# Attention: the products with ones of a key tile stand directly behind its value products, and not a step later

## The chip, the cores and the metric

The kernel runs on one core of a Trainium2 chip. The metric is the device time of one execution in microseconds (us), and the median of several runs is taken.

## The reference

A transformer block on x of 2 x 2048 x 512 in float32: x plus attention of the normalised x, and then a mixture of experts with a shared expert, which the change doesn't touch. What matters here is the attention, with 16 heads of 32 columns:

```python
scores = jnp.einsum('bhqd,bhkd->bhqk', q, k) / jnp.sqrt(jnp.float32(DH))
causal = jnp.tril(jnp.ones((s, s), dtype=bool))
scores = jnp.where(causal[None, None], scores, -jnp.inf)
attn = jax.nn.softmax(scores, axis=-1)
out = jnp.einsum('bhqk,bhkd->bhqd', attn, v)
```

## The kernel before

The program has three phases: projections (to about 275 us of the profiled execution), attention (to about 1435 us) and the experts. The order on every engine is written out by hand; semaphores tie the engines together.

Attention goes over 8 groups of four heads (`NG`; called rounds below). In a round it goes over four units, the query chunks q = 0 to 3 of 512 queries, and in a unit over the key tiles of 128 keys in the order `ORDER[q]`. A tile is two steps, one for each pair of heads, so there are 640 steps for 320 tiles. The last four key tiles by number of a unit (kt from 4q on) are diagonal tiles, which need the causal mask; `ORDER` spreads them among the full ones.

A step n of TensorE (PE) holds two score products (`score(n, 0)` and `score(n, 1)`, L1011, keys by queries, into one of three banks `b_st`), a share of the items of a stream (mostly L988: scores in the other orientation, queries by keys, into three banks `b_mx`, for the row maxima of a later unit), in thirds around the others, and in its middle one of two things:

- in odd steps, from the third on, the value group of the tile before, `values(m)`, L1024: four heads, each 32 columns wide in the array, side by side; a record of the trace says x8, since each head's float32 product is two instructions. It accumulates into the bank `b_ob`.
- in even steps the ones group of the same tile, `count_ones(m)`, L1038: the same exponentials (`b_pt`) multiplied by ones, which gives the softmax's row sums, into `b_sb`. It exists for 18 of a round's 40 tiles (`ONES_TILES`); for the others (`POOL_TILES`) GpSimd adds the exponentials up (L752), and at a unit's end `finish` (L1046) brings that sum into `b_sb`.

The other engines in a step: ScalarE (ACT) makes the exponentials of both scores (L931, `b_pt<-b_st`, eight buffers). On a diagonal tile both wait for VectorE (DVE), which adds the mask after both scores of the step are there (L893, or L897 in two pieces, `b_st<-b_st,b_sooner`). In DVE's order the mask stands behind the maxima (L871, L868) of the step's items of the first two thirds. PE's score number i (two to a step) waits until the exponential of number i - 3 has left the bank, and `values(m)` waits for the last exponential of its tile. ACT copies `b_sb` out for the unit that ended (L952) two or four steps into the next, and the first ones group of a unit waits for that copy (`s_sev`).

```python
ORDER = ((0, 1, 2, 3), (0, 1, 4, 2, 5, 3, 6, 7), (0, 1, 2, 8, 3, 4, 9, 5, 6, 10, 7, 11),
         (0, 1, 2, 12, 3, 4, 5, 13, 6, 7, 8, 14, 9, 10, 11, 15))
ONES_TILES = ((0, 1, 2, 3), (2, 6, 7), (2, 9, 6, 10, 11), (2, 4, 13, 8, 14, 15))
FINISH = (2, 4, 4, 2)
```

A group's width in columns is 512, less 128 for each tile that a diagonal tile lies behind the first diagonal one.

Of the kernel before, what the change touches and what calls it, by code (L numbers as in the profile page):

```python
# [604 lines left out]
def phase_attention(nc, x, w, scratch, ahead, keep, heads):  # L605
# [9 lines left out]
    NS, NU = len(steps), len(units)  # L615
# [22 lines left out]
    def item_shares(n):  # L638

        here, there = upto[n - 1] if n else start, upto[n]  # L640
        return [here + (there - here) * k // 3 for k in range(4)]
# [20 lines left out]
    def unit_ending(n, offset):  # L662

        for u in range(NU):
            if first_step[u + 1] + (offset[units[u][1]] if isinstance(offset, tuple) else offset) == n:
                return u
        return None

    with ExitStack() as ctx:
# [51 lines left out]
        with nc.Block() as block:  # L721
# [138 lines left out]
            def _(v):  # L860
                def partial_max(i):
                    _, u, t, h, c = stream[i]
                    q = units[u][1]
                    w = min(CH, (TPC * q + t + 1) * P - c * CH)
                    v.wait_ge(s_item, i + 1)
                    part = mpart[u % 2][:, t, h, c:c + 1]
                    if c == q:
                        v.tensor_tensor_reduce(unread[i % NMX][:, 0:w], mxb[i % NMX][:, 0:w], later[:, CH - w:], 1.0, -3e38,  # L868
                                               ALU.add, ALU.max, part).then_inc(s_red, 1)
                    else:  # L870
                        v.tensor_reduce(part, mxb[i % NMX][:, 0:w], AX.X, ALU.max).then_inc(s_red, 1)  # L871
                    if (t, h, c) == (TPC - 1, HG - 1, q):
                        v.wait_ge(s_red, maxes_before[i + 1])
                        v.tensor_reduce(mt[u % 2][:, :, 0:MROW + 1:DH], mpart[u % 2][:, :, :, 0:q + 1],
                                        AX.X, ALU.max, negate=True).then_inc(s_mcol, 1)
# [24 lines left out]
                for n in range(NS):  # L900
                    here, _, some, there = item_shares(n)
                    for i in range(here, some):
                        if stream[i][0] == "max":
                            partial_max(i)
                    if steps[n][2] >= TPC * steps[n][1]:
                        mask(n)
                    for i in range(some, there):
                        if stream[i][0] == "max":
                            partial_max(i)
                    if n == first_step[NQ * NG - 2]:  # L910
                        v.wait_ge(s_sum, 16)
                        v.reciprocal(rsum[:], sums[:]).then_inc(s_rec, 1)
# [57 lines left out]
            def _(pe):  # L970
                def item(i):
                    what = stream[i]
                    bank = mxb[i % NMX]
                    if i >= NMX:
                        if stream[i - NMX][0] == "max":
                            pe.wait_ge(s_red, maxes_before[i - NMX + 1])
                        else:
                            pe.wait_ge(s_turn, stream[i - NMX][1] + 1)
                    if what[0] == "max":
                        _, u, t, h, c = what  # L980
                        it, q = units[u]
                        w = min(CH, (TPC * q + t + 1) * P - c * CH)
                        if (t, h, c) == (0, 0, 0):
                            pe.wait_ge(s_q[q], 48 * (it + 1))
                        if (t, h) == (0, 0) and c == q:
                            pe.wait_ge(s_k[c][it % 2], 48 * (it // 2 + 1))
                        at = key_slot(it, c) * CH
                        ins = pe.matmul(bank[:, 0:max(w, 2 * P)], qb[0:KR, h, q * CH + t * P:q * CH + (t + 1) * P],  # L988
                                        kb[0:KR, h, at:at + max(w, 2 * P)], start=True, stop=True)
                        ins.then_inc(s_item, 1)  # L990
                    else:
                        u = what[1]
                        pe.wait_ge(s_mcol, u + 1)
                        for t in range(TPC):
                            ins = pe.transpose(bank[0:MROW + 1, t * P:(t + 1) * P], mt[u % 2][:, t, :], ident[:])
                        ins.then_inc(s_item, 1)

                def score(n, j):
                    u, q, kt, p = steps[n]
                    it = units[u][0]  # L1000
                    d = kt - TPC * q
                    lo = min(max(d, 0) * P, 2 * P)
                    if 2 * n + j >= NST:
                        pe.wait_ge(s_exp, 2 * n + j - NST + 1)
                    if n == first_step[2] and j == 0:
                        pe.wait_ge(s_rest, 1)
                    if n == first_step[u] and j == 0:
                        pe.wait_ge(s_row[q], 16 * (it + 1))
                    at = key_slot(it, kt // TPC) * CH + kt % TPC * P
                    h = 2 * p + j  # L1010
                    pe.matmul(stb[:, (2 * n + j) % NST, lo:], kb[:, h, at:at + P],  # L1011
                              qb[:, h, q * CH + lo:(q + 1) * CH], start=True, stop=True).then_inc(s_st, 1)

                def values(m):
                    u, q, kt, _ = steps[2 * m]
                    it = units[u][0]
                    lo = max(kt - TPC * q, 0) * P
                    pe.wait_ge(s_exp, 4 * m + 4)
                    if kt == ORDER[q][0] and u:
                        pe.wait_ge(s_oev, u)  # L1020
                    if q == kt // TPC and kt % TPC == 0:
                        pe.wait_ge(s_v[q], 16 * (it + 1))
                    for h in range(HG):
                        ins = pe.matmul(ob[h * DH:(h + 1) * DH, lo:], vbuf[:, kt, h * DH:(h + 1) * DH],  # L1024
                                        pt[(2 * m + h // 2) % NPB][:, h % 2, lo:],
                                        start=(kt == ORDER[q][0]), stop=(kt == ORDER[q][-1]))
                    ins.then_inc(s_pv, 1)

                def count_ones(m):
                    u, q, kt, _ = steps[2 * m]  # L1030
                    if kt in POOL_TILES[q]:
                        return
                    lo = max(kt - TPC * q, 0) * P
                    begin = ONES_TILES[q][0]
                    if kt == begin and u:
                        pe.wait_ge(s_sev, u)
                    for h in range(HG):
                        ins = pe.matmul(sb[h * DH:(h + 1) * DH, lo:], ones[:],  # L1038
                                        pt[(2 * m + h // 2) % NPB][:, h % 2, lo:],
                                        start=(kt == begin), stop=(kt == ORDER[q][-1] and not POOL_TILES[q]))  # L1040
                    ins.then_inc(s_one, 1)

                def finish(u):
                    pe.wait_ge(s_add, pool_total(u))
                    for h in range(HG):
                        ins = pe.matmul(sb[h * DH:(h + 1) * DH, :], ones[:], acc[summed.index(u) % 2][:, h],  # L1046
                                        start=False, stop=True)
                    ins.then_inc(s_fin, 1)
# [6 lines left out]
                for n in range(NS):  # L1055
                    here, *some = item_shares(n)
                    score(n, 0)
                    for i in range(here, some[0]):
                        item(i)
                    if n % 2 == 0 and n >= 4:  # L1060
                        count_ones((n - 4) // 2)
                    if n % 2 and n >= 3:
                        values((n - 3) // 2)
                    for i in range(some[0], some[1]):
                        item(i)
                    score(n, 1)
                    for i in range(some[1], some[2]):
                        item(i)
                    done = unit_ending(n, FINISH)
                    if done is not None and done in summed:  # L1070
                        finish(done)
                values(NS // 2 - 1)
                count_ones(NS // 2 - 2)
                count_ones(NS // 2 - 1)
                finish(NU - 1)

# [1079 lines left out]
```

## Time and profile before

| | |
|---|---|
| median of 3 runs | 2293.08 us (2290.29 to 2299.49) |
| profiled execution, time | 2301.97 us |
| profiled execution, span | 2300.3 us |
| TensorE matmul busy | 2139.7 us, 93% |
| VectorE busy | 1483.7 us, 64% |
| GpSimd busy | 1168.6 us, 51% |
| ScalarE busy | 1034.7 us, 45% |
| mean granted TensorE clock | 0.974 of full speed |

Busy time of an engine is the union of its instructions' durations. Ends of matmuls are modelled in the trace, so distances in this document are taken from start to start. A time in brackets in a row of the timeline is the idle time of the engine before it, and behind it stands what ended it. The change touches attention alone, which takes 1160 of the 2300 us.

### The profile page before, as it was taken

Reading aid. Unit: us, or ns where it says so; the run is one execution under the profiler, and the core shown is the slowest. Engines: PE = TensorE matmul, PEld = TensorE weight load, DVE = VectorE, ACT = ScalarE, POOL = GpSimd, SP = SyncE. Lnnn points to the kernel's source line nnn. Section 1 sums busy time; section 2 is a strip of 40 time slices with the busy share of each in tenths; the row PEclk is TensorE's granted clock in tenths of the full one; section 3 lists DMA queues with packets and bytes.
Section 4 is the critical chain, followed back from the end, with each engine's and each line's share of the span. In section 5 each row is a group of like instructions: output and inputs, shape, how many; then the busy total and the mean of one; then the engine's idle time right before and its main releaser. Section 6 shows DMA issues by size and latency. Waiting matters only on the chain. (4 is left out here: it accounts for less than half of the span.)

```text
span 2300.3 us, 32737 instructions
## 1 busy us (share of the span) xinstructions
PE 2139.7 (93%) x11865; PEld 1389.3 (60%) x11865; DVE 1483.7 (64%) x3323; ACT 1034.7 (45%) x1924; POOL 1168.6 (51%) x717
## 2 busy tenths in 40 slices
PE   6999899999999999999999988699998899999997
PEld 5777544444444444444444432577776798999896
DVE  3665786767767677777777760765657556565654
ACT  3333255555555555555555555322222334443433
POOL 1010166557465674656746557455563345465554
PEclk9999799999999999999999999899999899999999
DMA  5678711412213122161231200344432676767673
GB/s 169 233 264 257 194 31 38 93 33 69 67 38 93 29 67 72 38 153 29 68 71 38 73 17 19 124 147 129 147 111 80 235 242 196 237 227 249 215 225 115
DMA packets 172913, 283.69 MB, mean 123 GB/s; under 512 B 28622, under 2 KB 75214, under 8 KB 172752
## 3 DMA queue, kind: packets, MB, share of 16 engines
q1 hardware_dynamic: 151488, 219.09, 32.5%
q0 software_dynamic: 21264, 62.51, 8.2%
q8 instruction: 94, 1.54, 0.3%
q14 instruction: 67, 0.55, 0.1%
HBM read 196.22 MB, written 86.90 MB: 123 GB/s over the span
## 5 line engine op out<-in xcount | busy, mean ns | idle before, releaser
L931 ACT ACTIVATE b_pt<-b_st 128x512 f32<-128x512 f32 (+3 forms) x1280 | 612.5, 535 | 472.7 <-DVE b_st L893 187.6
L752 POOL TENSOR_TENSOR b_acc<-b_acc,b_pt 128x1024 f32<-128x1024 f32 (+1 forms) x256 | 592.9, 2346 | 214.3 <-ACT b_pt L931 213.7
L871 DVE TENSOR_REDUCE b_mpart<-b_mx 128x1 f32<-128x512 f32 x768 | 512.1, 686 | 184.8 <-PE b_mx L988 182.1
L1011 PE MATMUL b_st<-b_q,b_k 97*128 97x512 f32 (+2 forms) x1280 | 497.4, 402 | 57.5 <-ACT b_pt L931 54.0
L988 PE MATMUL b_mx<-b_k,b_q 96*128 96x512 f32 (+2 forms) x1280 | 508.9, 412 | 6.9 <-DVE b_mpart L871 3.3
L988 PEld LDWEIGHTS b_mx<-b_k,b_q 96*128 96x128 f32 x1280 | 248.4, 195 | 262.0 <-DVE b_mpart L871 148.9
L1011 PEld LDWEIGHTS b_st<-b_q,b_k 97*128 97x128 f32 x1280 | 242.3, 191 | 262.7 <-ACT b_pt L931 237.4
L1024 PE MATMUL b_ob<-b_pt,b_v 128*32 128x512 f32 (+3 forms) x2560 | 303.6, 547 | 1.1 <-ACT b_pt L931 1.1
L868 DVE CUSTOM_DVE_ANT_0 b_unread<-b_mx,b_later 128x384 bf16<-128x384 f32 (+3 forms) x512 | 244.5, 484 | 87.0 <-PE b_mx L988 86.3
L752 POOL TENSOR_TENSOR b_acc<-b_pt 128x1024 f32<-128x1024 f32 x48 | 113.5, 2379 | 263.0 <-ACT b_pt L931 263.0
L80 PE MATMUL c_fb<-e_w_split,e_xh 128*128 128x352 f32 x408 | 142.3, 349 | 1.4 <-DVE e_xl L1727 1.4
L2015 ACT ACTIVATE c_hh<-e_tb 128x384 fp32r<-128x384 f32 x71 | 34.9, 491 | 230.4 <-PE e_tb L2065 187.6
L82 PE MATMUL c_fb<-e_w_split,e_xh 128*128 128x352 f32 x408 | 133.2, 326 | 0.0
L81 PE MATMUL c_fb<-e_w_split,e_xl 128*128 128x352 f32 x408 | 133.0, 326 | 0.0
L893 DVE TENSOR_TENSOR b_st<-b_st,b_sooner 128x256 f32<-128x256 f32 x171 | 73.1, 428 | 65.8 <-PE b_st L1011 65.6
L1038 PE MATMUL b_sb<-b_pt,b_ones 128*32 128x512 f32 (+3 forms) x1152 | 114.9, 471 | 0.0
L2042 DVE TENSOR_TENSOR c_hl<-e_tb,c_hh 128x384 fp32r<-128x384 f32 x71 | 39.5, 557 | 102.8 <-ACT c_hh L2015 97.6
L1024 PEld LDWEIGHTS b_ob<-b_pt,b_v 128*32 128x32 f32 x2560 | 50.6, 108 | 90.0 <-issue 46.4
L1981 POOL DMA_INDIRECT out_dram<-c_x,entry x36 | 50.5, 1403 | 83.0 <-DVE c_x L2030 52.1
L1412 POOL DMA_INDIRECT scr_table<-c_entry,c_slot x64 | 75.1, 1173 | 25.2 <-issue 18.0
L1981 POOL DMA_INDIRECT out_dram<-c_x1k,entry x35 | 45.4, 1297 | 71.1 <-DVE c_x1k L2030 29.0
L1451 ACT ACTIVATE c_sg<-c_fb 128x512 f32<-128x512 f32 (+1 forms) x24 | 14.3, 597 | 147.2 <-PE c_fb L82 139.6
(296 smaller groups left out, 3818.0 us busy)
## 6 DMA issues: line engine op xcount, KB each, us to landing
b_q<-scr_qh SPq DMA_DIRECT2D x64, 256.0 KB, 4.5
b_k<-scr_kh SPq DMA_DIRECT2D x64, 256.0 KB, 4.1
sw_raw<-in_L_ffn_w_gate_dram SPq DMA_DIRECT2D x14, 704.0 KB
sw_raw<-in_L_ffn_w_up_dram SPq DMA_DIRECT2D x14, 704.0 KB
c_x_rows<-in_L_ffn_w_gate_dram SPq DMA_DIRECT2D x13, 704.0 KB
c_x_rows<-in_L_ffn_w_up_dram SPq DMA_DIRECT2D x13, 704.0 KB
a_xin<-in_L_attn_x_dram POOLq DMA_DIRECT2D x8, 1024.0 KB, 5.8
scr_qh<-wo SPq DMA_DIRECT2D x8, 1024.0 KB, 5.0
```

Source lines behind the costliest of these rows:

```text
L80: nc.tensor.matmul(out, wh, xh, start=first, stop=False)
L81: nc.tensor.matmul(out, wl, xh, start=False, stop=False)
L82: return nc.tensor.matmul(out, wh, xl, start=False, stop=last)
L752: g.tensor_tensor(out[:, :, lo:], so_far[:, :, lo:], pt[n % NPB][:, :, lo:], ALU.add).then_inc(s_add, 1)
L868: v.tensor_tensor_reduce(unread[i % NMX][:, 0:w], mxb[i % NMX][:, 0:w], later[:, CH - w:], 1.0, -3e38, ALU.add, ALU.max, part).then_inc(s_ ...
L871: v.tensor_reduce(part, mxb[i % NMX][:, 0:w], AX.X, ALU.max).then_inc(s_red, 1)
L931: act.activation(pt[n % NPB][:, j, lo:], stb[:, (2 * n + j) % NST, lo:], ACT.Exp, scale=SCALE).then_inc(s_exp, 1)
L988: ins = pe.matmul(bank[:, 0:max(w, 2 * P)], qb[0:KR, h, q * CH + t * P:q * CH + (t + 1) * P], kb[0:KR, h, at:at + max(w, 2 * P)], start=Tr ...
L1011: pe.matmul(stb[:, (2 * n + j) % NST, lo:], kb[:, h, at:at + P], qb[:, h, q * CH + lo:(q + 1) * CH], start=True, stop=True).then_inc(s_st, 1)
L1024: ins = pe.matmul(ob[h * DH:(h + 1) * DH, lo:], vbuf[:, kt, h * DH:(h + 1) * DH], pt[(2 * m + h // 2) % NPB][:, h % 2, lo:], start=(kt == ...
L1038: ins = pe.matmul(sb[h * DH:(h + 1) * DH, lo:], ones[:], pt[(2 * m + h // 2) % NPB][:, h % 2, lo:], start=(kt == begin), stop=(kt == ORDER ...
L1981: g.indirect_dma_start(out=out, in_=rows[i % RING], out_offset=at, in_offset=None, bounds_check=T - 1, oob_is_err=False).then_inc(s_sc, 16)
```

## The change

On PE the ones group of a tile leaves the even step and stands in the odd step before it, directly behind the tile's value group. Nothing is added or left out: 143 of the 144 ones groups move, and the last one of all stood there already. No other engine's order changes, and neither do the waits, the buffers or the shares of items that each step gets.

```diff
@@ -1057,10 +1057,9 @@
                     score(n, 0)
                     for i in range(here, some[0]):
                         item(i)
-                    if n % 2 == 0 and n >= 4:
-                        count_ones((n - 4) // 2)
                     if n % 2 and n >= 3:
                         values((n - 3) // 2)
+                        count_ones((n - 3) // 2)
                     for i in range(some[0], some[1]):
                         item(i)
                     score(n, 1)
@@ -1070,7 +1069,6 @@
                     if done is not None and done in summed:
                         finish(done)
                 values(NS // 2 - 1)
-                count_ones(NS // 2 - 2)
                 count_ones(NS // 2 - 1)
                 finish(NU - 1)
```

PE's order in the third round, unit q = 0, from the value group of tile 0 on, as it was. `b_ob` takes value groups, `b_sb` ones groups, `b_st` scores and `b_mx` items.

```order
L1024 MATMUL b_ob<-b_pt0,b_v 32x512 x2
L1024 MATMUL b_ob<-b_pt1,b_v 32x512 x2
L988 MATMUL b_mx2<-b_k,b_q 128x512
L1011 MATMUL b_st<-b_q,b_k 128x384
L988 MATMUL b_mx0<-b_k,b_q 128x512
L1011 MATMUL b_st<-b_q,b_k 128x256
L1038 MATMUL b_sb<-b_pt0,b_ones 32x512 x2
L1038 MATMUL b_sb<-b_pt1,b_ones 32x512 x2
L1011 MATMUL b_st<-b_q,b_k 128x256
L988 MATMUL b_mx1<-b_k,b_q 128x512
L1011 MATMUL b_st<-b_q,b_k 128x256
L1024 MATMUL b_ob<-b_pt2,b_v 32x384 x2
```

The same place of PE's order after the change.

```order
L1024 MATMUL b_ob<-b_pt0,b_v 32x512 x2
L1024 MATMUL b_ob<-b_pt1,b_v 32x512 x2
L1038 MATMUL b_sb<-b_pt0,b_ones 32x512 x2
L1038 MATMUL b_sb<-b_pt1,b_ones 32x512 x2
L988 MATMUL b_mx2<-b_k,b_q 128x512
L1011 MATMUL b_st<-b_q,b_k 128x384
L988 MATMUL b_mx0<-b_k,b_q 128x512
L1011 MATMUL b_st<-b_q,b_k 128x256 x2
L988 MATMUL b_mx1<-b_k,b_q 128x512
L1011 MATMUL b_st<-b_q,b_k 128x256
L1024 MATMUL b_ob<-b_pt2,b_v 32x384 x2
```

The ones group stood between the second and the third score behind the value group; now the two groups of eight are one block, and those two scores are neighbours.

## Rows read from the trace of the kernel before

**Rows 1.** The page: engine totals, TensorE clock granted in 40 slices of the span.

```profile
PE 2139.7 (93%) x11865; PEld 1389.3 (60%) x11865; DVE 1483.7 (64%) x3323; ACT 1034.7 (45%) x1924; POOL 1168.6 (51%) x717
PEclk9999799999999999999999999899999899999999
```

**Rows 2.** Waits of PE from 270 to 1430 us: total us, times, longest.

```profile
PE b_st L1011 <- ACT b_pt L931: 54.0, 108, 1.2
```

**Rows 3.** The page's groups: all ones groups (eight records each).

```profile
L1038 PE MATMUL b_sb<-b_pt,b_ones 128*32 128x512 f32 (+3 forms) x1152 | 114.9, 471 | 0.0
```

**Rows 4.** Timeline of PE, 706 to 708 us: start, duration, instruction.

```profile
706.04 0.39 PE L1011 MATMUL b_st<-b_q,b_k 97*128 97x512 f32 x1
706.36 1.07 PE L1024 MATMUL b_ob<-b_pt,b_v 128*32 128x512 f32 x8
707.36 0.50 PE L988 MATMUL b_mx<-b_k,b_q 96*128 96x512 f32 x1
707.70 0.40 PE L1011 MATMUL b_st<-b_q,b_k 97*128 97x512 f32 x1
707.93 0.34 PE L988 MATMUL b_mx<-b_k,b_q 96*128 96x384 f32 x1
```

**Rows 5.** Timeline of PE, 703 to 706 us: a ones group of 256 columns.

```profile
704.90 0.64 PE L1038 MATMUL b_sb<-b_pt,b_ones 128*32 128x256 f32 x8
705.47 0.50 PE L1011 MATMUL b_st<-b_q,b_k 97*128 97x512 f32 x1
```

**Rows 6.** Timeline of PE at the end of attention.

```profile
1428.26 0.43 PE L1024 MATMUL b_ob<-b_pt,b_v 128*32 128x128 f32 x8 [1.08 <-ACT b_pt L931]
1428.50 0.40 PE L1038 MATMUL b_sb<-b_pt,b_ones 128*32 128x128 f32 x8
```

**Rows 7.** Timeline, 577 to 581 us, round 3, q = 0, behind tile 0.

```profile
576.99 0.60 ACT L952 ACTIVATE b_sst<-b_sb 128x512 f32<-128x512 f32 x1
577.16 1.06 PE L1024 MATMUL b_ob<-b_pt,b_v 128*32 128x512 f32 x8
...
578.49 0.34 PE L1011 MATMUL b_st<-b_q,b_k 97*128 97x384 f32 x1
...
578.69 0.69 DVE L868 CUSTOM_DVE_ANT_0 b_unread<-b_mx,b_later 128x512 bf16<-128x512 f32 x1 [1.99 <-PE b_mx L988]
...
579.12 1.07 PE L1038 MATMUL b_sb<-b_pt,b_ones 128*32 128x512 f32 x8
...
579.31 0.49 DVE L897 TENSOR_TENSOR b_st<-b_st,b_sooner 128x128 f32<-128x128 f32 x2
...
579.92 0.87 ACT L931 ACTIVATE b_pt<-b_st 128x384 f32<-128x384 f32 x2 [2.33 <-DVE b_st L897]
580.46 0.39 PE L1011 MATMUL b_st<-b_q,b_k 97*128 97x256 f32 x1 [0.27 <-ACT b_pt L931]
```

**Rows 8.** Timeline, 650 to 652 us, q = 2, behind tile 6.

```profile
650.97 2.16 ACT L931 ACTIVATE b_pt<-b_st 128x256 f32<-128x256 f32 x5 [1.53 <-DVE b_st L893]
651.50 0.50 PE L1011 MATMUL b_st<-b_q,b_k 97*128 97x512 f32 x1
```

**Rows 9.** Timeline, 718 to 719 us, behind tile 15 of q = 3.

```profile
718.80 0.45 PE L1011 MATMUL b_st<-b_q,b_k 97*128 97x384 f32 x1 [0.35 <-ACT b_pt L931]
```

**Rows 10.** Windows, 465 to 470 us: length, busy time and count by engine, granted clock, DMA.

```profile
465.00:470.00 5.00, 5.00 (x24) 2.29 (x23) 2.53 (x6) 2.13 (x5) 0.00 (x0) 0.50 0.71 157
```

**Rows 11.** Timeline of PE: the same three tiles in round 2 and round 3.

```profile
463.10 0.39 PE L1011 MATMUL b_st<-b_q,b_k 97*128 97x256 f32 x1 [0.67 <-ACT b_pt L931]
...
463.69 0.64 PE L1024 MATMUL b_ob<-b_pt,b_v 128*32 128x256 f32 x8
...
478.92 1.06 PE L1024 MATMUL b_ob<-b_pt,b_v 128*32 128x512 f32 x8
...
611.78 0.64 PE L1024 MATMUL b_ob<-b_pt,b_v 128*32 128x256 f32 x8
...
622.58 1.06 PE L1024 MATMUL b_ob<-b_pt,b_v 128*32 128x512 f32 x8
```

## The prediction

> **What bounds the kernel now.** I read the page first: TensorE is busy for 93% of the span, VectorE for 64%, ScalarE for 45% [rows 1]. Then the waits of PE within attention: score products wait for ScalarE's exponentials for 54.0 us in 108 waits, and nothing else makes PE wait for more than a few us there [rows 2]. So attention is bound by PE's order. But the 54 us aren't spread evenly, and for this change it matters where they lie. So the third view is the timeline of PE, ScalarE and VectorE together, tile by tile. The rounds repeat each other almost to 0.1 us, so I went through one round (577 to 721 us) and read what stands behind each of its 18 ones groups.
>
> What the reader is to see there is the place behind tile 0 [rows 7]. The value group starts at 577.16. Behind it come an item and a score at 578.49, which is the second score of a diagonal step. Now a chain runs through other engines: VectorE takes the item's maximum (578.69, 0.69 us), then adds the mask (579.31), then ScalarE makes the exponential (from 579.92), and only then may PE write the score that needs this bank (580.46). PE has meanwhile done one more item, one score and the ones group (579.12). It still waits 0.27 us. So the ones group isn't on the path here: it is what PE does while the chain runs.
>
> **The change, part by part.** It removes two changes of shape on PE for each ones group, and it moves the group ahead of the chain.
>
> *What a change of shape costs.* Groups have the form 128\*32, all other products use the full width. Between two plain products of 512 columns the starts are 0.23 us apart (707.70 to 707.93). A plain product ahead of a group takes 0.32 (706.04 to 706.36), 0.09 more. A group of 512 takes 1.00 to the next plain product, and that one takes 0.34 to its successor, 0.11 more [rows 4]. A group of 256 takes 0.57 [rows 5], so 256 columns cost 0.43, and one of 128 would take 0.355 if a plain product followed. At the end of attention a ones group follows a value group of 128 directly, after 0.24 [rows 6]: 0.115 less. So where a ones group stands directly behind its value group, PE's own work is shorter by 0.09 + 0.11 + 0.115 = 0.31 us. The page's 1152 records are 144 groups [rows 3]. The page "TensorEngine Tiling (Array Packing)" of the Trainium skill, section Key Properties, says that changing the tiling mode drains the engine; the trace agrees, with 0.31 us for the way in and out, and by that rule alone the change could only gain.
>
> *What the move costs.* The block of both groups is longer than the value group by what a group takes in front of another one: 1.00 - 0.115 = 0.885 us at 512 columns, 0.67 at 384, 0.455 at 256, 0.24 at 128. All that stands behind the block starts so much later, the item and the second score of the step among them, and with them the chain through mask and exponential. In front of the waiting score there is now no group. So the wait comes to light in full.
>
> I take the 18 places of a round by what comes next. The wait that a place already has, or the slack it has, decides how much of the delay is seen.
>
> - *Four places with a 512 group ahead of a diagonal tile that is the first or second one* (behind tile 0 of q = 0 and tile 2 of the other three units). The score waits for the exponential already, or starts within 0.1 us of its end, as in rows 7. The chain and this score start 0.885 later. The score no longer follows a group, which gives 0.11 back: +0.775 each, 3.10 together. Does another part of the chain absorb some? VectorE had been idle for 1.99 us before the item came [rows 7], so no.
> - *Four places ahead of a later diagonal tile* (tiles 1 and 2 of q = 0, 6 of q = 1, 6 of q = 2). The mask is narrower, and there is slack between the exponential's end and the score. Behind tile 6 of q = 2 the exponentials start at 650.97; one of 256 columns takes about 0.4, so the score at 651.50 was free some 0.09 earlier [rows 8]. That gives 0.885 - 0.09 - 0.11 = +0.685. For the three others, read the same way, slack is 0, 0.05 and 0.05 with groups of 384, 256 and 256: +0.56, +0.295, +0.295. Together 1.84.
> - *Two more places ahead of a diagonal tile* (8 and 15 of q = 3). Here an earlier wait for the exponential of the step before absorbs the delay of the block. Behind tile 15 the later score waits 0.35 anyhow [rows 9], and I count 0. Behind tile 8 the gain in PE's work remains: -0.31.
> - *Eight places ahead of a full tile.* No mask; the exponential is made within the time of the next three scores and their items, also 0.885 later. The gain in PE's work is seen: -0.31 for seven. The eighth (tile 9 of q = 2) has six items, and VectorE's 0.69 for each maximum [rows 7] holds it: I count -0.12. Together -2.29.
>
> A round: 3.10 + 1.84 - 0.31 - 2.29 = +2.34 us; eight rounds: **+18.7 us**. Nothing hides later what was lost: PE's order continues behind the wait as it was.
>
> *Other edges.* The move frees `b_pt` a step earlier; ScalarE doesn't wait for ones groups in any row that I found, so this is worth nothing. The first ones group of a q = 0 unit now meets its wait for ScalarE's copy of the sums: the copy starts at 576.99 and takes 0.60, the ones group would start 0.885 after 577.16, at 578.05, 0.46 after the copy [rows 7]. Queued behind it would be everything of PE. I take 0. The queues of SP and GpSimd aren't moved past.
>
> *Against which time.* The rows come from an execution of 2301.97 us (span 2300.3, 1.7 outside it); with the sum it would take 2320.7. The median of the runs is 2293.08, 8.9 lower. So the forecast is 2293.1 + 18.7 = about 2312 us.
>
> *Bounds.* If the eight gains came without any delay being seen, and -0.31 at all 144, the sum would be -44.6 us. If the gains failed and the delays held, 8 x 4.94 = +39.5. If only half of each delay is seen, 8 x (2.47 - 2.60) = -1.
>
> **The rivals.**
>
> 1. *PE's work is all that counts* (faster). For it: 93% busy, 54 us of waits against 1160, and 0.31 us less work at each of 144 places. Against it: the waits stand just where the groups are moved from. It decides if the chain can be repaid, that is if the time from the block's end to the waiting score is shorter than I read it by more than 0.5 us. Time: 2293.1 - 44.6 = 2248.5.
> 2. *A wash.* The chain is shorter behind a long block, since ScalarE and VectorE have cleared all their older work by then, and half the delay is absorbed. For it: ScalarE still has up to two older exponentials when a value group starts. Against it: VectorE idle for 1.99 and ScalarE for 2.33 us in rows 7. Time: 2293.1 - 1 = about 2292.
> 3. *The clock.* From 465 to 470 us the granted clock is 0.50, the lower level of 1.2 GHz [rows 10], where most of attention has 1.00 (2.4 GHz). Ahead of it PE had waited 0.67 us for an exponential. The stretch from 463.69 to 478.92 takes 15.23 us, the same tiles a round later 10.80 [rows 11]: 4.4 us for one such episode. The page's clock row shows few such slices [rows 1]; read finely, attention has three after its start. The change adds some 32 waits of about a microsecond. If each round got one more episode, that is 8 x 4.4 = 35 us on top: 2347. Against it: behind each long wait there now stands no longer gap than those that the rounds have five times each already, mostly with the full clock. The page "TensorE: Matmul & The Clock Gate", in the section on why this matters for kernels, advises against idle gaps between bursts since the clock falls with them; the trace agrees that the clock falls after a stretch with waits, here one of 0.67 us.
> 4. *The sums' copy is late*, and PE stands at the first ones group of seven q = 0 units. It decides from 0.46 us on; 0.5 us beyond that would be 3.5 us. I count it inside the range and not by itself.
>
> **How the numbers follow.** Forecast as summed, 2301 to 2326: 0.60. Rival 1: 0.10. Rival 2: 0.18. Rival 3: 0.12. The range of eight in ten is 2297 to 2335: below it lie rival 1 and most of rival 2, above it rival 3's larger half. A difference under 0.5%, 11.5 us, is about what a measurement of this kernel can't tell from none; slower by more is the forecast and rival 3 (0.72), within it rival 2 (0.18), faster rival 1 (0.10).
>
> **What the profile of the changed kernel would show.** Right, if a ones group of 512 starts about 0.885 us behind its value group; if PE's waits of scores for exponentials rise from 54 us by some 60 (the delays seen, and the 0.31 at each of these places, which becomes waiting) and stand at the third score behind the blocks ahead of diagonal tiles, 1.1 us more at each of the four places of the first kind; if the distance from the value group of tile 0 to that of tile 1 in q = 0 grows by 0.8, and the one behind tile 14 of q = 3 falls by 0.3; and if a round without a fall of the clock takes about 2.3 us longer. Wrong, if the ones group behind its value group costs more than 0.885 (then it is worse), if the mask starts earlier after the block than the item's maximum lets it (then rival 1 or 2), or if the windows show more than three stretches at half the clock.

## The result, and the profile after

The changed kernel takes 2332.95 us (median of 4 executions, 2328.25 to 2340.85), where the kernel before has 2295.89 beside it: a ratio of 1.0169, 95% interval 1.0137 to 1.0202. That is 31 to 46 us slower; 18.7 were forecast. The profiled execution took 2330.91 us with a span of 2329.2. One execution of all that follow, of the kernel joined ahead of full tiles, took 4129 us at a mean clock of 0.528 and is left out of the ratios.

The page after, engine totals and the clock granted in 40 slices [rows 1]:

```profile
PE 2116.9 (91%) x11865; PEld 1403.3 (60%) x11865; DVE 1474.5 (63%) x3323; ACT 1029.8 (44%) x1924; POOL 1167.7 (50%) x717
PEclk9999799999999999999999999799999899999999
```

Waits of PE in attention after, 270 to 1462 us (total us, times, longest) [rows 2]:

```profile
PE b_st L1011 <- ACT b_pt L931: 109.9, 147, 1.3
```

PE has the same instructions and is busy for 23 us less, and it waits for exponentials for 56 us more; some 60 were forecast. The forty slices don't show the clock's falls, which are a few us long; that comes below.

The place of [rows 7] in the timeline after, behind tile 0 of q = 0 in the third round (start, duration, instruction):

```profile
580.54 0.60 ACT L952 ACTIVATE b_sst<-b_sb 128x512 f32<-128x512 f32 x1
580.72 1.07 PE L1024 MATMUL b_ob<-b_pt,b_v 128*32 128x512 f32 x8
581.60 1.04 PE L1038 MATMUL b_sb<-b_pt,b_ones 128*32 128x512 f32 x8
...
582.91 0.34 PE L1011 MATMUL b_st<-b_q,b_k 97*128 97x384 f32 x1
...
583.11 0.69 DVE L868 CUSTOM_DVE_ANT_0 b_unread<-b_mx,b_later 128x512 bf16<-128x512 f32 x1 [2.85 <-PE b_mx L988]
...
583.73 0.49 DVE L897 TENSOR_TENSOR b_st<-b_st,b_sooner 128x128 f32<-128x128 f32 x2
...
584.33 0.87 ACT L931 ACTIVATE b_pt<-b_st 128x384 f32<-128x384 f32 x2 [3.19 <-DVE b_st L897]
584.88 0.39 PE L1011 MATMUL b_st<-b_q,b_k 97*128 97x256 f32 x1 [1.27 <-ACT b_pt L931]
585.10 0.41 PE L988 MATMUL b_mx<-b_k,b_q 96*128 96x512 f32 x1
...
585.57 0.53 PE L1024 MATMUL b_ob<-b_pt,b_v 128*32 128x384 f32 x4
```

Counted from the start of the value group, the ones group starts at 0.88 (0.885 forecast), and all links of the chain stand 0.85 or 0.86 later than before: the second score at 2.19 (1.33), the mask at 3.01 (2.15), the exponentials at 3.61 (2.76), the waiting score at 4.16 (3.30). PE's own work reaches that score 1.27 us too early. The sums' copy ends at 581.14, before its ones group starts, as forecast.

Since the rounds repeat each other, I compared both traces by places: the distance from one value group's start to the next, for each of a round's 40 tiles, as the median over the rounds. 22 tiles without a ones group: within 0.01 us of before. The 18 with one, in us of change, beside the forecast:

| places of a round | forecast | measured |
|---|---|---|
| 512 columns, ahead of the first or second diagonal tile (4) | +0.775 each, +3.10 | +0.88, +0.89, +0.87, +0.85, together +3.49 |
| ahead of a later diagonal tile (4) | +0.56, +0.295, +0.295, +0.685, together +1.84 | +0.65, +0.31, +0.26, +0.80, together +2.02 |
| behind tiles 8 and 15 of q = 3 | -0.31, 0 | -0.19, +0.01 |
| ahead of a full tile (8) | -2.29 together | -0.34, -0.33, +0.06, -0.08, -0.27, -0.20, -0.21, -0.20, together -1.57 |
| a round | +2.34 | +3.76 |
| eight rounds | +18.7 | +30.1 |

The total attention stretch, first to last value group, grew by 33.5 us (1153.5 to 1187.0). So 30 are in the places; the rest is in rounds that the medians leave out, those with falls of the clock among them. The two other phases are together 4.6 us shorter in this profile than in the one before, which is why the spans differ by only 29.

### The profile page after: what moved, and what is told of

It is laid out like the page before. It is cut to its first block and busy times, and to the rows that moved or that the text cites. A ratio compares the mean times of both kernels' runs of the same rounds, so it can differ in the third digit from the quotient of the medians.

```text
span 2329.2 us, 32737 instructions
## 1 busy us (share of the span) xinstructions
PE 2116.9 (91%) x11865; PEld 1403.3 (60%) x11865; DVE 1474.5 (63%) x3323; ACT 1029.8 (44%) x1924; POOL 1167.7 (50%) x717
## 5 line engine op out<-in xcount | busy, mean ns | idle before, releaser
L1011 PE MATMUL b_st<-b_q,b_k 97*128 97x512 f32 (+2 forms) x1280 | 487.6, 400 | 112.7 <-ACT b_pt L931 109.9
L80 PE MATMUL c_fb<-e_xh,c_sw_guh 128*128 128x512 f32 (+2 forms) x192 | 77.0, 401 | 3.7 <-DVE e_xl L1567 3.7
```

Of the source, the lines that this page charges most:

```text
L80: nc.tensor.matmul(out, wh, xh, start=first, stop=False)
```

## The experiments

All are set against the kernel before, run beside them on the same chip. "Joined" means that a ones group stands directly behind its value group.

**Joined only ahead of full tiles.** `mask_next(m)` says whether the tile after m is diagonal.

```diff
-                    if n % 2 == 0 and n >= 4:
+                    if n % 2 == 0 and n >= 4 and mask_next((n - 4) // 2):
                         count_ones((n - 4) // 2)
                     if n % 2 and n >= 3:
                         values((n - 3) // 2)
+                        if not mask_next((n - 3) // 2):
+                            count_ones((n - 3) // 2)
```

> The ones group joins its value group only where the next key tile is a full one (8 of 18 places of a round); where the next tile is diagonal it stays a step later. Theory (the ones group covers the mask chain of the next tile; PE's own work is shorter at each joined place): 8 places give what they gave in the changed kernel, together -1.57 us a round, so -12 to -14 us against before, about 0.994 of it. Rival A (a longer block of two groups costs by itself, at any place, since ScalarE and VectorE run dry during it): slower than before by 8/18 of the loss, +15 us. Rival B (the loss is the clock): about -18 plus what the clock takes, no change of the distances at the ten other places either way.

Measured: ratio 0.997 (0.995 to 0.999), median 2290.24 against 2296.98, 7 us faster. The eight places read -0.34, -0.32, +0.06, -0.08, -0.27, -0.20, -0.19, -0.21, as in the changed kernel, and none of the other 32 moved by over 0.03. Rival A, that a long block costs by itself, is out for these places: 8 of a round's 18 blocks are here, and the kernel is faster. Only one of the eight has groups of 512 columns, so for the long blocks the kernels without mask below decide. The places sum to -12 us, and 5 of these are missing in the median.

**Joined only ahead of diagonal tiles**, the complement (the two conditions swapped).

> The complement: joined only at the ten places of a round where the next tile is diagonal. Theory: +5.3 us a round, +43 us against before, more than the whole change, whose loss is this less the gain at the eight other places; a PE wait of 1.1 to 1.3 us for an exponential at the third score behind each block of 512 columns. Rival A: +20 us, ten eighteenths of the loss. If the two parts don't add up to the whole change (+31 in attention, clock apart), places act on one another.

Measured: 1.0181 (1.0142 to 1.0219), 2339.14, 42 us slower. The places: +0.88, +0.65, +0.31, +0.85, +0.26, +0.86, +0.80, +0.86, -0.19, a round +5.3, eight rounds +42. The two parts don't act on each other: each place reads the same, within 0.05 us, whether the others are joined or not, and -7 and +42 give +35, inside the interval of the whole.

**Ahead in the order, but behind the second score.** Neither before nor after the change: the ones group stands in the value group's step, directly behind that step's second score. The edit is shown against the changed kernel.

```diff
                     if n % 2 and n >= 3:
                         values((n - 3) // 2)
-                        count_ones((n - 3) // 2)
                     for i in range(some[0], some[1]):
                         item(i)
                     score(n, 1)
+                    if n % 2 and n >= 3:
+                        count_ones((n - 3) // 2)
```

> All ones groups move ahead in the order, but not past the second score behind the value group: they stand in the same odd step as the value group, directly behind that step's second score. No change of shape is saved. Theory (what counts is that the ones group stands behind the score which the mask waits for and ahead of the score which waits for the exponential): within 5 us of before, either way, and the distance from value group of tile 0 to that of tile 1 in q = 0 stays at 3.9 to 4.1 us. Rival C (any move of the ones group ahead costs, in proportion to what it passes): about half of the changed kernel's loss, +18 us.

Measured: 1.0029 (1.0004 to 1.0053), 2301.19, 4 us slower by the medians and 7 by the ratio; by places only one of 40 moved by over 0.03 (tile 9 of q = 2, by +0.24, 2 us in all). So moving the group ahead, but only to right behind the second score, costs next to nothing, and moving it across that score too costs the 30 us. What counts is the side of the score on which the chain begins.

**Two ones groups a tile later, as cover.** If a ones group hides a chain, one that hides nothing should be worth most where a chain has no cover.

```diff
+                def late(m):
+                    u, q, kt, _ = steps[2 * m]
+                    return (q, kt) in ((3, 4), (2, 10))
...
-                    if n % 2 == 0 and n >= 4:
+                    if n % 2 == 0 and n >= 6 and late((n - 6) // 2):
+                        count_ones((n - 6) // 2)
+                    if n % 2 == 0 and n >= 4 and not late((n - 4) // 2):
                         count_ones((n - 4) // 2)
```

> No group is joined. Two of a round's ones groups move to a later place: that of tile 4 of q = 3 and that of tile 10 of q = 2 stand one tile later, where PE waits behind a value group for the mask chain of a diagonal tile and no ones group stands. Theory: there the group takes the place of waiting (idle and lost time of 1.2 and 0.8 us), and its old place gets shorter by its own price with the changes of shape (1.2 and 0.76): -1.9 us a round, -15 us. Rival D (PE's work decides, waits are merely moved): no change, 0 +-3.

Measured: 0.9944 (0.9926 to 0.9962), 2285.60, 11 to 13 us faster. By places -1.05 behind tile 4 of q = 3 and -0.51 behind tile 10 of q = 2, -12.5 us in eight rounds, where 15 were expected. The timeline of PE in this kernel, behind tiles 4 and 5 of q = 3:

```profile
674.80 1.07 PE L1024 MATMUL b_ob<-b_pt,b_v 128*32 128x512 f32 x8
675.80 0.50 PE L988 MATMUL b_mx<-b_k,b_q 96*128 96x512 f32 x1
...
677.60 1.06 PE L1024 MATMUL b_ob<-b_pt,b_v 128*32 128x512 f32 x8
...
679.68 1.06 PE L1038 MATMUL b_sb<-b_pt,b_ones 128*32 128x512 f32 x8
680.68 0.39 PE L988 MATMUL b_mx<-b_k,b_q 96*128 96x256 f32 x1
680.90 0.48 PE L1011 MATMUL b_st<-b_q,b_k 97*128 97x512 f32 x1
...
682.22 0.85 PE L1024 MATMUL b_ob<-b_pt,b_v 128*32 128x384 f32 x8
```

The same place in the kernel before, behind tile 5:

```profile
684.22 1.06 PE L1024 MATMUL b_ob<-b_pt,b_v 128*32 128x512 f32 x8
...
687.51 0.50 PE L1011 MATMUL b_st<-b_q,b_k 97*128 97x512 f32 x1 [1.01 <-ACT b_pt L931]
...
688.84 0.53 PE L1024 MATMUL b_ob<-b_pt,b_v 128*32 128x384 f32 x4
```

The distance behind tile 5 is 4.62 with the ones group in it and 4.62 without: it took the place of the 1.01 us of waiting and of what PE loses around it. Behind tile 4, where it had stood, the distance fell from 3.85 to 2.80. Rival D, that waits are only moved, is out.

**The chain taken away.** Two kernels that leave out the causal mask: VectorE adds none, ScalarE waits for the score.

```diff
-                    if steps[n][2] >= TPC * steps[n][1]:
-                        mask(n)
...
-                        if kt >= TPC * q:
-                            act.wait_ge(s_msk, masked(n) + 1)
-                        else:
-                            act.wait_ge(s_st, 2 * n + j + 1)
-                        act.activation(pt[n % NPB][:, j, lo:], stb[:, (2 * n + j) % NST, lo:], ACT.Exp, scale=SCALE).then_inc(s_exp, 1)
+                        act.wait_ge(s_st, 2 * n + j + 1)
+                        act.activation(pt[n % NPB][:, j, lo:], stb[:, (2 * n + j) % NST, lo:], ACT.Exp, scale=0.001 * SCALE).then_inc(s_exp, 1)
```

With the groups apart, as before:

> The order of before, but VectorE adds no causal mask and ScalarE waits for the score alone; the exponential's scale is a thousandth, so that nothing overflows. It leaves out the mask. The base for the next kernel. Theory: the waits behind value groups ahead of diagonal tiles vanish (five places of a round at about 1.0 us, some more at the others), -40 to -60 us against before.

With the groups joined, as changed:

> The changed kernel with the same mask left out and the same scale. Theory (the loss is the mask chain, which the ones group covered): with no chain the places ahead of diagonal tiles behave like those ahead of full ones, -0.2 to -0.3 us each, so 25 to 40 us faster than the kernel without mask and with the groups apart. Rival A (a long block starves ScalarE, whatever the mask): slower than that kernel, by 15 us or more.

Measured: 2224.68 apart (0.9701 of before, 68 us less, where 40 to 60 were expected) and 2198.98 joined (0.9589). So without the mask the same change gives -25.7 us. The four wide places, which cost 0.85 to 0.89 each with the mask, give -0.19, -0.30, -0.31 and -0.26; the eight places of the first two kinds together give -2.35 a round where they cost +5.51. All places together give -4.2 a round, which over eight rounds is 8 us more than the -25.7. The six middle rounds show it (-4.0 to -5.7 each); the first has only -2.2 and the last +0.4, and why these two give less stays open. PE behind tile 0 of q = 0 in the joined kernel without mask:

```profile
548.59 1.06 PE L1019 MATMUL b_ob<-b_pt,b_v 128*32 128x512 f32 x8
549.48 1.04 PE L1033 MATMUL b_sb<-b_pt,b_ones 128*32 128x512 f32 x8
550.45 0.50 PE L983 MATMUL b_mx<-b_k,b_q 96*128 96x512 f32 x1
...
551.20 0.40 PE L1006 MATMUL b_st<-b_q,b_k 97*128 97x256 f32 x2
```

The second and third scores behind the block stand together (551.20, x2), with no wait between. This shows the cause: the loss is the mask chain behind a longer block, and not the length of the block.

**The changed kernel again**, for a narrower interval.

> The changed kernel again, for a narrower interval. By the distances of its places +3.78 us a round, +30.2 in attention; with the clock's share of the first profile +33.5. Theory: 2327 to 2331 where before has 2297. If it stays at +37 or more, 4 to 7 us are outside the places of attention that were read.

Measured: 1.0177 (1.0151 to 1.0204), 2338.47, 41 us slower than 2297.63. The places read as in the first profile, but for the one behind tile 5 of q = 1, to which I come back. So about 10 us are outside them, and my theory had no room for that. What differed between executions was the mean granted clock: 0.9697 on average here, 0.9744 in the executions of before. Over 46 executions of the kernel before, in three series, the clock runs from 0.968 to 0.979 and the time from 2308 to 2288, close to a line of 1.7 us for each 0.001. The difference of 0.0047 is worth 8 us by it, if the line holds for the changed kernel too. It also explains the missing 5 us of the first experiment in part: its clock was 0.9728 against 0.9747, 3 us.

**Waits filled.** Is it the waiting that makes the clock fall? This kernel is the changed one, with the item behind a block's second score multiplied several times into the same bank.

```diff
-                def item(i):
+                def item(i, times=1):
...
-                        ins = pe.matmul(bank[:, 0:max(w, 2 * P)], qb[0:KR, h, q * CH + t * P:q * CH + (t + 1) * P],
-                                        kb[0:KR, h, at:at + max(w, 2 * P)], start=True, stop=True)
+                        for _ in range(times):
+                            ins = pe.matmul(bank[:, 0:max(w, 2 * P)], qb[0:KR, h, q * CH + t * P:q * CH + (t + 1) * P],
+                                            kb[0:KR, h, at:at + max(w, 2 * P)], start=True, stop=True)
...
+                def filled(n):
+                    u, q, kt, p = steps[n]
+                    _, before, was, _ = steps[max(n - 3, 0)]
+                    if n % 2 == 0 or n < 3 or was not in ONES_TILES[before] or (q, kt) == (0, 0):
+                        return 1
+                    return {0: 4, 1: 4, 2: 2}.get(kt - TPC * q, 1)
...
                     for i in range(some[1], some[2]):
-                        item(i)
+                        item(i, filled(n) if i == some[1] else 1)
```

> The changed kernel, with TensorE given idle work inside the waits: the item behind the second score of a block is multiplied three times more into the same bank (once more ahead of a third diagonal tile), 0.7 us of the 1.3 us of waiting. Nothing else changes. If the long waits are what makes the clock fall more often in the changed kernel: distances as in the changed kernel, mean granted clock back from about 0.970 to 0.974 or more, and 5 to 9 us faster than the changed kernel on the same chip. If something else makes it fall: clock and time as the changed kernel's within 2 us. If the extra products cost (no room in the wait): slower by up to 20 us.

Beside it on the same chip the changed kernel a third time:

> The changed kernel beside it on the same chip: 2331 to 2340 at a mean granted clock of 0.969 to 0.973; at equal clock 30 to 33 us above before.

Measured: 2327.97 with the waits filled (1.0133, 1.0111 to 1.0155), 2339.63 without (1.0192, 1.0167 to 1.0216). More work on PE, 12 us less time, where 5 to 9 were expected. The mean clock is 0.9770 and 0.9698, without overlap between the executions (0.975 to 0.978, 0.966 to 0.972). PE behind tile 0 in the filled kernel:

```profile
578.19 1.07 PE L1025 MATMUL b_ob<-b_pt,b_v 128*32 128x512 f32 x8
579.08 1.04 PE L1039 MATMUL b_sb<-b_pt,b_ones 128*32 128x512 f32 x8
...
580.57 1.08 PE L989 MATMUL b_mx<-b_k,b_q 96*128 96x512 f32 x4
581.49 0.28 PE L1012 MATMUL b_st<-b_q,b_k 97*128 97x256 f32 x1
582.36 0.39 PE L1012 MATMUL b_st<-b_q,b_k 97*128 97x256 f32 x1 [0.59 <-ACT b_pt L931]
...
583.05 0.53 PE L1025 MATMUL b_ob<-b_pt,b_v 128*32 128x384 f32 x4
```

The distance to the next value group is 4.86, in the changed kernel 4.85. Over all places a round differs from the changed kernel's by 0.02 to 0.04 us. So the gain is the clock: 0.0072 more of it is 12 us by the line. With the waits filled the change costs 30.1 us by the medians (26 to 36 by the ratio), at a clock 0.0014 above that of before; the places say 30.1.

**A version that is faster than both**: joined ahead of full tiles, except for the two groups that move later as cover. The edit is the first and the fourth together.

> The two versions that gained, together: groups joined where the next tile is full, except that of tile 4 of q = 3 and that of tile 10 of q = 2, which move a tile later as cover. From the places measured so far: -0.34 -0.32 +0.06 -0.27 -0.19 -0.21 (six joined) and -1.05 -0.51 (two moved) = -2.8 us a round, -22.6 us against before. If the joined places gain less in sum than place by place, as in the earlier run (-7 measured, -12 by places), about -18.

Measured: 0.9917 (0.9894 to 0.994), 2277.42 against 2297.63. The medians of the places sum to -2.46 a round, -19.7 us, and the measured difference is 20. The two agree partly by chance: +0.28 of that sum stands behind tile 0 of q = 2, where no group moved and three later rounds are longer by 0.5 to 1.1. Without it the places say -2.7 a round, -22 us.

**The same with the remaining waits filled**, `filled` returning 3 ahead of tiles 4 and 6 of q = 1 and 9 of q = 2.

> The version with groups joined and two moved as cover, plus idle products (the item behind the second score, twice more) in the three places of a round where PE still waits behind a value group without a ones group: ahead of tiles 4 and 6 of q = 1 and 9 of q = 2. If waits make the clock fall: clock from 0.974 to 0.977 or above and 3 to 5 us off that version's 2277, so 2272 to 2275. If the clock in it falls for other reasons: 2277 +-2. Distances of places unchanged in either case.

Measured: 0.9923 (0.9905 to 0.9941), 2278.27, clock 0.9753, with 0.9752 in before beside it. No gain shows. But 3 to 5 us were expected and the interval is 4 us wide to either side, so a gain of that size isn't excluded; whether the falls that are left in that version come from these three waits is open.

## Why the forecast was right in kind and off in size

**What bounds it.** Right: PE's order, and the chain of score, mask and exponential behind a value group as the place where its waiting lies. The two experiments with a part of the change, the one behind the second score and the two without mask each show it.

**The price of a change of shape.** Right: 0.31 us. Eight of the ten places ahead of diagonal tiles give -0.26 to -0.34 when there is no mask; the other two give -0.19 and +0.02.

**The delay of the block.** Right: 0.88 for 0.885.

**"The score no longer follows a group, which gives 0.11 back."** Wrong; this is the step that failed inside the chain terms. The waiting score costs its successor as much after a wait as after a group: in the fence of the changed kernel above it starts at 584.88, and the item behind it stands 0.22 later (585.10). A product of that width in unbroken succession needs 0.12. The kernel before shows the same at 512 columns, with no ones group near, behind tile 5 of q = 3: 0.33 where 0.23 is usual [rows 4].

```profile
681.95 0.19 PEld L1011 LDWEIGHTS b_st<-b_q,b_k 97*128 97x128 f32 x1
682.18 0.33 PE L1011 MATMUL b_st<-b_q,b_k 97*128 97x384 f32 x1
...
687.51 0.19 PEld L1011 LDWEIGHTS b_st<-b_q,b_k 97*128 97x128 f32 x1 [1.34 <-ACT b_pt L931]
687.51 0.50 PE L1011 MATMUL b_st<-b_q,b_k 97*128 97x512 f32 x1 [1.01 <-ACT b_pt L931]
687.84 0.40 PE L988 MATMUL b_mx<-b_k,b_q 96*128 96x512 f32 x1
...
704.45 0.28 PE L988 MATMUL b_mx<-b_k,b_q 96*128 96x256 f32 x1
704.57 0.40 PE L1011 MATMUL b_st<-b_q,b_k 97*128 97x512 f32 x1
```

So the first product after a wait pays the 0.11 too, as the first after a group does. The rows of PEld (the loading of a product's weights) show what both have in common: in succession the weights start to load 0.23 ahead of their product (681.95 for 682.18), after a wait only together with it (687.51), as after a group. No run tests whether this makes the 0.11. It was credited at eight places of a round: 7 us over the kernel. The two chain terms together measure 0.57 a round above their forecasts, 4.6 us: by places the 0.11 shows at six of them, in full or in part.

**The eight places ahead of full tiles.** Right in sign, too large: -1.57 for -2.29, 5.8 us over eight rounds. I had let three scores and their items take up a delay of 0.885, and at six of the eight places they don't quite. The changed kernel behind tile 4 of q = 3:

```profile
688.45 1.07 PE L1024 MATMUL b_ob<-b_pt,b_v 128*32 128x512 f32 x8
689.33 1.04 PE L1038 MATMUL b_sb<-b_pt,b_ones 128*32 128x512 f32 x8
...
691.10 0.51 PE L1011 MATMUL b_st<-b_q,b_k 97*128 97x384 f32 x2
691.45 0.40 PE L988 MATMUL b_mx<-b_k,b_q 96*128 96x512 f32 x1
691.72 0.44 PE L1011 MATMUL b_st<-b_q,b_k 97*128 97x384 f32 x1
692.09 0.64 PE L1024 MATMUL b_ob<-b_pt,b_v 128*32 128x512 f32 x4
```

The score at 691.72 is held a little by its exponential (which ends at 691.67 in the trace), and as a first product after a wait it takes 0.37 to the value group, where 384 columns took 0.26 in the trace before. That is the same 0.11 again. Behind tiles 13 and 14 of q = 3 and 10 of q = 2 a score that its exponential holds also costs 0.11 more to what follows; tiles 4, 13 and 14 of q = 3 give -0.20 for -0.31 each. The place behind tile 9 of q = 2 gives +0.06 for -0.12. For all this the trace alone speaks; no experiment took it apart.

**The two places of q = 3.** -0.18 for -0.31 together, 1 us.

**Rival 3, the clock.** I had given it 0.12 and priced it at 35 us, and the sum put it at nothing. It is there and smaller: the executions of the changed kernel lie at a mean clock 0.0047 and 0.0058 below before in the two larger series, 8 to 10 us by the line, and 12 us came back when the waits were filled. One of its falls, in the windows of the changed kernel (length, busy time and count by engine, granted clock, DMA):

```profile
755.00:760.00 5.00, 3.80 (x27) 1.54 (x16) 2.55 (x6) 2.58 (x6) 3.33 (x2) 0.90 0.02 3
760.00:765.00 5.00, 4.85 (x27) 2.49 (x19) 3.08 (x8) 1.26 (x3) 4.94 (x3) 0.76 0.00 0
765.00:770.00 5.00, 3.88 (x39) 2.27 (x42) 3.23 (x10) 2.85 (x9) 0.09 (x1) 1.00 0.26 73
```

and what PE did ahead of it, in the timeline:

```profile
758.03 0.50 PE L1011 MATMUL b_st<-b_q,b_k 97*128 97x512 f32 x1 [1.20 <-ACT b_pt L931]
...
759.28 1.51 PE L1024 MATMUL b_ob<-b_pt,b_v 128*32 128x384 f32 x8
```

A wait of 1.20 us, then a value group that takes 1.44 to the next product where one of its width takes 0.78 at full clock. Such a fall costs one to two us, while the one that I had priced took 4.4; it stands at the half clock for some 3.4 us, the priced one for some 10. The profile of the changed kernel has eight falls in attention, all of the short kind, that of the kernel before three, the filled one three. More than three was a sign of being wrong that the prediction had named.

The falls aren't spread by chance. This one stands behind tile 5 of q = 1, after the block of tile 2 and its long wait. The distance there is 2.62 in most rounds, and 3.7 to 4.0 in two rounds of the first profile of the changed kernel, in three of the second and in four of the third. In the kernel before and in the filled one no round does this, but for the first, which has 3.19 in every kernel. Five of the eight falls of the changed kernel I read one by one, and each has a wait of 0.94 to 1.26 us for an exponential ahead of it. In the filled kernel's profile attention spends some 10 us at the half clock, in the changed one beside it some 44.

What I can't settle: the kernel joined only ahead of diagonal tiles has the same long waits and yet a mean clock of 0.9742 in four executions, close to before. The kernel joined only ahead of full tiles has no longer waits and yet 0.9728, and without the mask joining took the clock from 0.9762 to 0.9745. Waits are a cause, since filling them restored the clock, but which of them count, and what the blocks ahead of full tiles add, stays open.

**Rivals 1 and 2.** Neither came about. Without the mask rival 1 is what happens, at 60% of its price (25.7 for 44.6).

The sum, by its own terms: 18.7 forecast, +4.6 at the chain places, +1.0 at the two of q = 3, +5.8 at the full ones, together 30; and 7 to 12 for the clock, which the sum did not hold. So what failed is the 0.11 credited after a wait, the delay taken as absorbed ahead of full tiles, and the clock at nothing; the mechanism stood.

## What to carry to other kernels

Before two groups of products are joined to save changes between them, look at what the second one hides: a product that stands in the shadow of another engine's chain is free where it is, and moving it ahead of the chain's first link delays the chain by its full length. Time such places by the distance of equal instructions over repeated rounds, since medians of a whole kernel can't show 0.3 us. And price a wait at more than its length: here it also cost 0.11 us at the next product, and with many of them the clock fell.

## What was not expected of the hardware

The first product after a wait pays the same 0.11 us to its successor (0.33 for 0.23 at 512 columns) as the first after a change of shape. With waits of up to 1.3 us among dense work TensorE's mean granted clock stood at 0.9698 where the kernel before had 0.9756, and idle products in those waits brought it to 0.9770 and the time down by 12 us. Some of the falls came back at the same place of a round in three profiles, behind a wait of 1.20 us.
